# Output projection in two halves, q/k scaling on two engines, evictions in another order, in one attention + expert kernel

## What is computed

```python
h = ln(x) + (silu(t) @ W_ada.T + b_ada)
qkv = (h @ Wqkv.T).reshape(b, n, 3, H, HD)            # B, N, D = 16, 256, 256; H, HD = 16, 64
q, k = ln(qkv[:, :, 0]), ln(qkv[:, :, 1])             # per head, over HD
attn = softmax(q @ k.T / sqrt(HD))
x = x + (attn @ v).reshape(b, n, H * HD) @ Wout.T     # the output projection
gate = softmax(x @ Wgate.T); vals, idx = top_k(gate.T, 512)
y = gelu(ln(x[idx]) @ fc1.T + b1) @ fc2.T + b2        # per expert
out = x.at[idx].add(y * vals)
```

## Time and profile before

| | |
|---|---|
| median of 3 runs | 1306.81 us (1305.21 to 1308.42) |
| the profiled execution | 1306.09 us, span 1304.3 us |
| mean granted TensorE clock | 0.932 |
| TensorE matmul busy | 1092.4 us, 84% |
| VectorE busy | 937.3 us, 72% |
| ScalarE busy | 714.8 us, 55% |
| GpSimd busy | 532.6 us, 41% |
| transfers | 37 GB/s over the span |

### The profile page before, as it was taken

The page is one execution under the profiler, slowest core; times in us unless marked ns, Lnnn a source line. Parts: engine busy times, 40 slices in busy tenths (PEclk is TensorE's granted clock), DMA queues, the critical chain, the costliest instruction groups (busy, mean ns, idle before and its releaser), DMA issues.

```text
span 1304.3 us, 23806 instructions
## 1 busy us (share of the span) xinstructions
PE 1092.4 (84%) x7843; PEld 873.6 (67%) x7843; DVE 937.3 (72%) x1744; ACT 714.8 (55%) x1970; POOL 532.6 (41%) x468
## 2 busy tenths in 40 slices
PE   7888987988889888888988989889897304999996
PEld 6567676766667676767676767667674204898896
DVE  5787777777686767777777777786765685777773
ACT  5665656556565656565656566565654100554541
POOL 2444444434354444454444444353544003335423
PEclk9889899989999998999899989999997655999998
DMA  5000000000000100000000000000000413335512
GB/s 177 1 9 18 17 18 17 16 16 16 16 20 12 32 16 16 16 16 16 16 16 16 16 16 16 16 16 9 25 18 9 170 13 107 100 104 166 126 17 33
DMA packets 31772, 48.58 MB, mean 37 GB/s; under 512 B 7920, under 2 KB 28528, under 8 KB 30448
## 3 DMA queue, kind: packets, MB, share of 16 engines
q1 hardware_dynamic: 25584, 39.49, 9.3%
q0 software_dynamic: 6144, 8.52, 3.6%
HBM read 35.29 MB, written 12.71 MB: 37 GB/s over the span
## 4 chain that ended last, share of the span: by engine, by line
PE 60%; DVE 19%; issue 11%; ACT 6%; POOL 1%; DMA 1%; DVEq 0%; ACTq 0%; SPq 0%; POOLq 0%
PE ch L483 10%; PE av L1418 9%; PE ch L485 8%; PE ch L484 8%; PE sc L1356 6%; PE mx L1396 6%; DVE probT L1204 5%; ACT prob L1058 3%; PE pq L1383 3%; DVE qn L862 2%; DVE bn L1123 1%; DVE hit L735 1%; DVE m L1234 1%; PE sc L483 1%; PE sc L485 1%
## 5 line engine op out<-in xcount | busy, mean ns | idle before, releaser
L947 POOL TENSOR_TENSOR prob<-prob,inverse 128x1024 f32<-128x1024 f32 x128 | 242.7, 1896 | 383.9 <-DVE inverse L1209 383.7
L1058 ACT ACTIVATE prob<-sc,m 128x256 f32<-128x256 f32 x512 | 235.5, 476 | 88.8 <-DVE m L1234 88.7
L1204 DVE COPY probT<-mx 128x1024 f32<-128x1024 f32 x128 | 156.5, 1223 | 102.1 <-PE mx L1396 100.9
L1234 DVE TENSOR_REDUCE m<-sc 128x4 f32<-128x1024 f32 x128 | 156.0, 1218 | 97.4 <-PE sc L1356 97.3
L952 POOL TENSOR_TENSOR qk_lo<-qkT,qk_hi 128x512 fp32r<-128x512 f32 x128 | 164.1, 1282 | 150.2 <-ACT qk_hi L1052 146.0
L483 PE MATMUL ch<-w_hi,hT_lo 128*128 128x512 f32 x384 | 175.3, 457 | 0.9 <-DVE hT_lo L1197 0.9
L1418 PE MATMUL av<-probT,V 128*64 128x256 f32 x1024 | 145.1, 406 | 35.5 <-DVE probT L1204 33.5
L485 PE MATMUL ch<-w_hi,hT_hi 128*128 128x512 f32 x384 | 156.1, 406 | 0.0
L484 PE MATMUL ch<-w_lo,hT_hi 128*128 128x512 f32 x384 | 155.8, 406 | 0.0
L1396 PE MATMUL mx<-con,prob 128*128 128x128 f32 x1024 | 144.3, 287 | 6.2 <-POOL prob L947 6.1
L862 DVE TENSOR_TENSOR qn<-raw,rstd 128x512 f32<-128x512 f32 x128 | 103.9, 872 | 50.6 <-POOL rstd L924 50.6
(11 more groups left out here) (194 smaller groups left out, 2543.4 us busy)
## 6 DMA issues: line engine op xcount, KB each, us to landing
fcw<-experts SPq DMA_DIRECT2D x8, 2048.0 KB
...
```

Source lines behind the costliest of these rows:

```text
L947: nc.gpsimd.tensor_tensor(pr, pr, r, ALU.mult).then_inc(normalised, 1)
L1058: ins = nc.scalar.activation(prob[hp % 2][:, g * N:(g + 1) * N], sc[:, g * N:(g + 1) * N], ACT.Exp, bias=m[hp % 2][:, g:g + 1], scale=-1.0 ...
L1204: nc.vector.tensor_copy(probT[:, :], mx[:, :]).then_inc(probT_ready, 1)
L1234: nc.vector.tensor_reduce(m[hp % 2][:, :], sc[:, :].rearrange("p (g n) -> p g n", n=N), AX.X, ALU.min).then_inc(max_ready, 1)
```

## The change

1. **Projection.** The 48 matmuls become two halves of 24, one for each four head pairs, and each half two quarters of 12 (`project`). In pair 6 TensorE makes head pairs 0 and 1 ahead of `av` and 2 and 3 behind the gate, of the current batch; in pair 2 of the next batch 4 and 5 ahead of `av` and 6 and 7 behind the scores. Scores now stand behind `av` in all pairs. Each half fills a bank of its own: VectorE adds the first into `xr_sb` in place (pair 7), and the second to that sum, giving `tok` (pair 3). What depends on `tok` follows: its statistics in pair 4, `xh2` in pair 7, its store to `out` behind the count of pair 3.
2. **Banks.** `tokT` and gate share one slot, so the slots stay 16 a batch.
3. **Scaling.** VectorE scales the first two of four parts of q and k, GpSimd the other two, one in pairs 1 and 5 behind the refinement, one in pairs 2 and 6. The refinement now stands ahead of `qk_lo`. VectorE's part moves from the end of pair 1 to pair 2; in pair 6 it stands behind `qkT` and no longer ahead.
4. **Evictions and orders.** ScalarE evicts the second chunk of a pair in the next pair, behind the next `qkT`, and makes `power_guess` behind `qk_hi`. On VectorE `qkT` comes right behind the reciprocal, the sums of squares of the first chunk behind `o_lo`; `hT_hi` and `hT_lo` at the end of pair 2.

```diff
@@ batch_slots, make_counts
-        out += [(1, 3, "wout", "dve"), (6, 0, "tokT", "act"), (6, 1, "gate", "dve")]
+        out += [(2, 0, "wout_second", "dve"), (6, 0, "tokT", "act"), (6, 1, "gate", "dve")]
+    if cur:
+        out += [(6, 2, "wout_first", "dve")]
@@ gpsimd
+            def scale(b, hp, c):
+                g = b * 2 + (1 if hp == 0 else 2)
+                par = 1 if hp == 0 else 0
+                need(rstd_ready, through("newton", b, hp))
+                need(qk_transposed, (g - 1) * GU)
+                times_rstd(nc.gpsimd, par, c).then_inc(qn_others_ready, 1)
...
+                    if hp == 1 and cur:
+                        refine(b, 0)
+                        scale(b, 0, 2)
+                    if hp == 5 and (nxt or prv) and not (isinstance(b, int) and b == B):
+                        refine(b, 4)
+                    if hp == 5 and nxt:
+                        scale(b, 4, 2)
+                    if hp == 2 and cur:
+                        scale(b, 0, 3)
+                    if hp == 6 and nxt:
+                        scale(b, 4, 3)
                     if (cur and nxt) or (cur and hp < UNITS - 1) or (nxt and hp == UNITS - 1):
 
                         need(hi_ready, u + 2)
                         need(scored, u)
                         nc.gpsimd.tensor_tensor(qk_lo[par][:, :], qkT[par][:, :], qk_hi[par][:, :].bitcast(F32), ALU.subtract).then_inc(lo_ready, 1)
-                    if hp == 1 and cur:
-                        refine(b, 0)
@@ vector
-                for c in range(4):
-                    ins = times_rstd(1 if hp == 0 else 0, c)
+                for c in range(2):
+                    ins = times_rstd(nc.vector, 1 if hp == 0 else 0, c)
...
+                    if hp == 3 and prv:
+                        need(slot_filled, through("slot", b, (2, 0)))
...
+                        nc.vector.tensor_tensor(flat_rows(tok), flat_rows(xr_sb), ch[slot_bank(b, (2, 0))][:, :], ALU.add).then_inc(dve_read, 1)
+                    if hp == 7 and cur:
+                        need(slot_filled, through("slot", b, (6, 2)))
+                        need(xr_in, (b + 1) * 16)
+                        nc.vector.tensor_tensor(flat_rows(xr_sb), flat_rows(xr_sb), ch[slot_bank(b, (6, 2))][:, :], ALU.add).then_inc(dve_read, 1)
@@ tensor
+            def project(bank, pairs, last):
+                for pair in pairs:
+                    for t in range(TT):
+                        ins = three_passes(bank[:, t * D:(t + 1) * D], o_hi[:, pair, t * P:(t + 1) * P], o_lo[:, pair, t * P:(t + 1) * P],
+                                           wo_hi[:, pair, :], wo_lo[:, pair, :], pair % GU == 0 and t == 0, pair % GU == GU - 1 and t == TT - 1)
+                if last:
+                    ins.then_inc(slot_filled, 1)
...
                         need(qn_ready, b * 2 + (hp + 1) // GU + 1)
+                        need(qn_others_ready, 2 * (b * 2 + (hp + 1) // GU + 1))
...
-                    if cur and hp in (2, 6):
-                        scores(u, hp % 2)
+                    if hp == 2 and prv:
+                        second = take_bank(b, (2, 0))
+                        need(o_split, u - 4)
...
+                        project(second, (4, 5), False)
+                    if hp == 6 and cur:
+                        first = take_bank(b, (6, 2))
...
+                        project(first, (0, 1), False)
...
-                    if hp == 1 and prv:
-                        bank = take_bank(b, (1, 3))
...
+                    if hp == 2 and prv:
+                        need(o_split, u - 2)
+                        project(second, (6, 7), True)
+                    if hp == 6 and cur:
+                        need(o_split, u - 2)
+                        project(first, (2, 3), True)
```

More of the change, by code:

```diff
@@ L91, in make_counts @@
             hit(who, b, key)
-            slots.append((b, key, who))
+            if name == "gate":
+                slots[-1] = (b, (6, 0), who, key)
+            else:
+                slots.append((b, key, who, key))
             if name in ("q", "k"):
@@ L100, in make_counts @@
                 hit(kind, b, 0)
-    for n, (b, key, who) in enumerate(slots):
-        table["bank", b, key] = n % 2
-        table["index", b, key] = n
+    for n, (b, key, who, last) in enumerate(slots):
+        table["bank", b, key] = table["bank", b, last] = n % 2
         if n >= 2:
-            pb, pkey, pwho = slots[n - 2]
-            table["free", b, key] = (pwho, table[pwho, pb, pkey])
+            pb, _, pwho, plast = slots[n - 2]
+            table["free", b, key] = (pwho, table[pwho, pb, plast])
     return table
@@ L1008, in chunk, with shifted_rows @@
                     nc.scalar.activation(V[1 if hp in ODD_STEPS else 0][:, t, :], bank[:, :], ACT.Copy).then_inc(act_read, 1)
+            def shifted_rows(b):
+                need(slot_filled, through("slot", b, (1, 2)))
+                need(bias1_ready, 1)
+                need(hT_split, b + 1)
+                bank = ch[slot_bank(b, (1, 2))]
+                for c in range(DC):
+                    bias = (bias1[:, c, b + 1:b + 2] if isinstance(b, int) else bias1[:, c, bass.ds(b + 1, 1)])
+                    ins = nc.scalar.activation(hT[:, c, :], bank[:, c * N:(c + 1) * N], ACT.Identity,
+                                               bias=bias, scale=vec[:, LN1_G + c:LN1_G + c + 1])
+                ins.then_inc(act_read, 1)
             def batch(b, cur, nxt, prv):
+                entry = isinstance(b, int) and b < 0
                 for hp in range(UNITS):
@@ L1019, in batch @@
                         need(lo_ready, u)
-                        if isinstance(b, int) and b < 0:
+                        if entry:
                             need(q_vec_ready, 1)
@@ L1045, in batch @@
                         if hp == 2 and prv:
-                            need(slot_filled, through("slot", b, (1, 3)))
+                            need(slot_filled, through("slot", b - 1, (6, 2)))
+                        if hp == 6 and prv:
+                            need(slot_filled, through("slot", b, (2, 0)))
                         nc.scalar.activation(o_hi[:, (hp - 2) % UNITS, :], av[:, 0:N], ACT.Copy).then_inc(o_hi_ready, 1)
+                    if live and values:
+                        chunk(b, hp, 0)
                     if ahead:
@@ L1052, in batch @@
                         nc.scalar.activation(qk_hi[par][:, :], qkT[par][:, :], ACT.Copy).then_inc(hi_ready, 1)
+                    if hp == 1 and cur:
+                        power_guess(b, 0)
+                    if hp == 5 and (nxt or prv) and not (isinstance(b, int) and b == B):
+                        power_guess(b, 4)
+                    if entry and hp == 5:
+                        weights_high(1, 1)
                     if cur:
@@ L1060, in batch @@
                         ins.then_inc(prob_ready, 1)
-                    if live:
-                        chunk(b, hp, 1)
-                    if hp == 1 and nxt:
-                        need(slot_filled, through("slot", b, (1, 2)))
-                        need(bias1_ready, 1)
-                        need(hT_split, b + 1)
-                        bank = ch[slot_bank(b, (1, 2))]
-                        for c in range(DC):
-                            bias = (bias1[:, c, b + 1:b + 2] if isinstance(b, int) else bias1[:, c, bass.ds(b + 1, 1)])
-                            ins = nc.scalar.activation(hT[:, c, :], bank[:, c * N:(c + 1) * N], ACT.Identity,
-                                                       bias=bias, scale=vec[:, LN1_G + c:LN1_G + c + 1])
-                        ins.then_inc(act_read, 1)
             over_batches(act, batch)
@@ L1192, in batch @@
                         shift()
-                    if hp == 2 and nxt:
-                        need(act_read, through("act", b, (1, 2)))
-                        chain(nc.vector.tensor_copy(hT_hi[:, :, :], hT[:, :, :]))
-                        nc.vector.tensor_tensor(hT_lo[:, :, :], hT[:, :, :], hT_hi[:, :, :].bitcast(F32), ALU.subtract).then_inc(hT_split, 1)
-                    if isinstance(b, int) and b < 0 and hp == 2:
+                        split_rows(b)
                         low_parts(0, 1)
@@ L1420, in batch @@
                         ins.then_inc(attended, 1)
-                    if cur and hp not in (2, 6):
+                    if cur:
                         scores(u, hp % 2)
```

123 lines of the change are left out of this document (63 added, 60 removed).

## The result

The changed kernel takes 1221.96 us, the median of 4 runs (1217.93 to 1225.16); beside it the kernel before took 1306.28 us (1305.21 to 1308.42). The ratio is 0.9351, interval 0.932 to 0.9382. The forecast was 1220. The profiled execution took 1221.37 us, span 1219.6.

What follows compares the result with a forecast made beforehand. TensorE's work plus its waits bound the kernel: 51.9 + 0.9 + 1.8 + 0.9 + 0.3 gave a 55.8 us pass, 5.6 less, 15 times, plus 2.9 at the end: 1220 us. Range 1190 to 1245 (60%), 1182 to 1266 (8 in 10).

Steps and rivals of the forecast that it cites:

- The pass: One batch's loop pass: 61.4 us before, 55.8 after, from 51.9 of TensorE work plus waits; gain 5.6.
- The bank waits: TensorE waits for the bank V stood in, ahead of each projection half in pairs 2 and 6: 0.9 us each.
- The wait of 2.56 us in pair 6: TensorE's late `pq`, with VectorE's `qkT` behind four scalings: goes, as `qkT` comes first and TensorE has more work before.
- The collision in pair 2: VectorE's scalings wait for GpSimd's multiply and scaling on the shared port; TensorE waits 1.8 us, ends 0 and 3.1.
- GpSimd's scaling: Time of one 128x512 scaling on GpSimd: 1.1 us, estimated between 1.03 and 1.28.
- small waits: Further short TensorE waits in a pass: 0.3 us, estimated from the 0.4 for a normalised tile before.
- The last stretch: Attention's end, without chunks: 24 of 48 projection matmuls leave it, a gain of 2.9 us.
- The clock: Pair 7's half clock, costing every second pass 1.2 us, goes because no wait of 2.56 us is left.
- A: Lock goes against VectorE: pair 3 waits 3.1 us, pair 6 is 1.3 late; pass 58.4, total 1258 us; 17%.
- B: TensorE nearly full: no collision in pair 2, bank waits at low ends; pass 53.1, total 1178 us; 13%.
- C: Clock halves behind the new waits in pairs 2, 3 and 6; pass 63.7, total 1338 us; 7%.
- D: Waits only move, with GpSimd's `qn` late for `pq` in pairs 3 and 7; about 1300 us; 3%.

Runs made afterwards that it cites:

- experiment 6: Kernel before with VectorE's k half of `qkT` moved ahead of the scalings, in all pairs; 1330.16 us, 1.0165.
- experiment 1: Kernel before with only the projection in halves (and `tok`, its statistics and the bank table with it); 1297.6 us, 0.9921.
- experiment 2: Changed kernel with the whole projection back in pair 1, V of pairs 1 and 5 evicted ahead of the next `qkT`; 1345.44 us, 1.0289.
- experiment 5: Changed kernel with all four scalings on VectorE, at the places of the change; 1245.45 us, 0.9522.
- experiment 9: Changed kernel with the `xh2` rows of pair 7 behind `m` and `o_lo` on VectorE; 1209.58 us, 0.9245.
- Experiment 8: Kernel before with the gate's eight matmuls made three times over, same result; 1313.17 us, 1.0037.
- experiments 1 to 3: The parts apart: halves alone 1297.6 us, whole projection with new orders and split scaling 1345.44 us, split scaling alone in the kernel before 1328.45 us.
- the best kernel here: Changed kernel with `xh2` behind `m` and `o_lo`, V evicted ahead of `qkT` (pairs 1, 5), `hT_hi` and `hT_lo` of pair 2 ahead of `o_lo`; 1202.55 us.

## Why the prediction was right, step by step

**The pass, 55.8 as predicted.** TensorE's work was counted right for full pairs and pairs 1 and 7 (6.74 and 6.29 predicted, 6.67 and 6.24 measured). Pairs 2 and 6 were priced too low: they have 6.56 and 7.89 us of TensorE busy, where 6.15 and 7.6 were counted. Of the 0.7 more, 0.55 is the four quarters, which take 1.5 to 1.6 us each and not 1.44, since each begins with a matmul of up to 0.39 us; the rest is the end of the transposes ahead of the bank waits, which nothing overlaps. Pair 3 has 0.17 more for the same reason. So the work of a pass is 52.7 us and not 51.9, and the waits are 3.1 and not 3.9. The row of the full-clock pass had shown this: 52.73 busy.

**The bank waits**, 0.9 each: 0.88 and 0.88.

**The wait of 2.56 us in pair 6** went. The forecast gave two reasons. That `qkT` comes first on VectorE isn't one: put first in the kernel before, it made the wait longer (experiment 6). That TensorE has the second quarter of the projection to do ahead of that `pq` is: with the halves alone, `qkT` still behind four scalings, the wait is gone (experiment 1).

**The collision in pair 2**, 1.8 us in pair 3 predicted, 0.55 measured. The mechanism was right: VectorE waits for the multiply (1.6 us; 1.7 predicted), and one GpSimd scaling (1.04) comes between its two. But the instructions hand over without the 0.4 us that was added; a VectorE scaling holds the other engine up for 0.45, less than its 0.60 from start to start. So VectorE's chain from `probT` to the end of `hT_lo` takes 7.8 us and not 8.7, while TensorE's work beside it was 7.4 and not 7.0. The collision came out 1.25 us cheaper; the dearer work (0.8) and the wait in pair 0 that the forecast had not counted (0.49) use that up. That the pass is 55.8 to a tenth is luck.

**GpSimd's scaling**, 1.1 estimated between 1.03 and 1.28: alone it takes 1.04, the lower end, to 0.01.

The Trainium skill (SBUF — State Buffer, section "SBUF: two separate sides") says of the port pair that VectorE and GpSimd share that whoever starts first gets it for the whole instruction; the trace agrees with that in 3.63 us for two scalings. Who is next when both wait, the forecast had left open; in experiments 2, 5 and 6 and in the changed kernel they alternated wherever GpSimd had its next instruction ready.

**What the forecast missed.** The wait of 0.49 us in pair 0: the move of `xh2` to pair 7 was named in the change and never priced; experiment 9 shows it (12 us over the program, of which 6 lie in the 13 passes). `xr_sb` in pair 7 cost nothing, as said. Pairs 4 and 5 have 0.14 of wait each, together the 0.3 of small waits. The first batch was to gain 5.6 and gained 0.8: the first `rstd` comes at 30.1 us instead of 24.4, since ScalarE's first guess now stands behind a V eviction that waits 2.6 us for its chunk. The last stretch gained 8.1, with 2.9 expected; its mean clock is 0.91 instead of 0.78. These errors cancel too: -4.8, +5.2, -1.4 behind the last `tok`, -1.2 in the other stretches, against a forecast of 87 and a result of 84.7. So the total, 2 us from the forecast, is closer than its terms were.

**The clock.** That the half clock of pair 7 would go was right, but the reason given (no wait of that length left) isn't shown. Experiment 8 has a short wait and the half clock, which begins ahead of the wait; the changed kernel has short waits and full clock in all passes. In other kernels the clock fell in or just behind a wait in every pass: 3.4 us at `av` with the halves alone, 2.2 at `pq` in experiment 2, 2.05 at `pq` with the split alone.

**The rivals.** A (the lock goes against VectorE) happened in part in other kernels: `qk_lo` did get in between four scalings (experiments 5 and 6). B needed collision and bank waits both gone; the best kernel here, with passes of 54.5, is 1.4 us above its 53.1. C did not come in the changed kernel (1.00 in the whole loop), but its mechanism did, in every pass of experiments 1 to 3. D was the right thing to fear: with the split alone the waits only move.

**What carried the gain.** The order of the shares matters, so no part has one price:

| projection | scaling | orders | us | ratio | a pass: TensorE busy + idle |
|---|---|---|---|---|---|
| whole | VectorE | old | 1306.28 | 1 | 54.0 + 7.4 |
| whole | split | old | 1328.45 | 1.0154 | 55.6 + 7.6 |
| whole | split | new | 1345.44 | 1.0289 | 55.4 + 9.4 |
| halves | VectorE | old | 1297.60 | 0.9921 | 55.2 + 6.1 |
| halves | split | old | 1228.82 | 0.9395 | 52.5 + 3.8 |
| halves | VectorE | new | 1245.45 | 0.9522 | 53.0 + 4.3 |
| halves | split | new | 1221.96 | 0.9351 | 52.7 + 3.1 |

The last column is the mean of ten passes, `tok` 4 to `tok` 14, in the profiled executions. With the split, and with the new orders, the refinement stands ahead of `qk_lo`; in the third row V of pairs 1 and 5 is evicted earlier than in the change.

The split costs 1.5% with the whole projection and gains 5.3% with the halves. The new orders gain 4.0% with all scalings on VectorE, 0.4% with the split, and cost 1.3% with the whole projection. The halves give pairs 2 and 6 the length in which VectorE and GpSimd can take their turns; the split or the orders bring `probT` of pair 2 sooner once pair 1 no longer covers it (the wait at `av` is 3.39 with the halves alone, 1.66 with the split, none with the new orders). And the clock multiplies this: the four kernels with 54 us of TensorE busy or more ran part of their passes at half clock, the three with halves and split or orders did not. Of the 5.0 us a pass between halves alone and halves with split, 2.7 is busy time and 2.3 waiting. Why the clock falls in one kernel and not in the other is not shown. Not tried: the whole projection with the new orders and all scalings on VectorE.
